# One VectorE pass of an attention kernel takes over the clamp, and the weighed values reach x by way of GpSimd

## The chip, the cores and the metric

The kernel runs on one core of one Trainium2 chip, as a single launch. The metric is the device time of that core in microseconds (us); lower is better. The time before the change is the median of three runs.

## The reference

x has 8 sequences of 512 tokens of 128 features. The reference computes x + 0.5 FFN(LN(x)), then x + Attention(LN(x)), then x + 0.5 FFN(LN(x)) again. The FFN is a mixture of 8 experts, two of them chosen per token. Only the attention matters here. It has 16 heads with complex queries and keys of 64 dimensions, turned by a phase. For a query i and a key j of a head, with dt = |i - j|:

```
E      = exp(clip(-mu * dt, -30, 0))
s      = Re(q_i . conj(k_j));  qn = |q_i|^2;  kn = |k_j|^2
V      = sigma_sq / (2 mu) * (1 - E*E) + eta_sq + gamma_sq
maha   = max(qn + E*E*kn - 2*E*s, 0) / V
logits = coef * log1p(maha / nu) - 0.5 * DH * log(V)      (masked where j > i)
out    = softmax(logits) @ v,   x = x + out @ Wo
```

## The kernel before, in words

There are three stages: a dense stage (an FFN, and preparation for the attention), the attention, and a second dense stage. All of them are written by hand for five queues (TensorE, VectorE, ScalarE, GpSimd and the SyncE queue, which issues the DMAs), with semaphores between them. On each queue the order is the order of the program text.

The attention stage walks through 128 pairs of a head and a sequence, head by head, eight sequences per head. Every queue has a function `a_step(i, r)`, called for steps -1 to 132; in step n = 16 i + r it works on several pairs at different depths of the pipeline. The score matrix of a pair is 512 x 512, of which only the lower triangle of 128 x 128 blocks is kept: four row blocks of 128, 384, 512 and 256 columns (in this order in memory), 1280 columns for each of the 128 partitions. In step n:

- TensorE: scores of pair n into `pS` (`scores`, L1186), norms of pair n+1 (`norms`), the projections of pair n+2 into `pQK` (`project`), the transposes of the probabilities of pair n-1 back into `pS` (`turn`, L1226; its two halves wait for the two halves of `t_done` of pair n, since they overwrite the same `pS`), in every second head the values for two heads (`values`, L1236), then the product of probabilities and values of pair n-2 into `p7` (`weigh`, L1300, which waits for `acc_done`, since `p7` is a single buffer).
- VectorE: `peaks` of pair n-1 (L1569: four instructions at L1578 that add `lam` and take the row minimum), the first half of `accumulate` of pair n-3 (L1603: x += p7 * rinv, two of four row tiles, L1609), `distances` of pair n (L1583: a pass pS = -2 pS + ek, L1587, and a second one u = pS * decay in two instructions of 512 and 768 columns, L1591), the transpose of the query norms of pair n+1 (L1597), the other half of `accumulate`, the phase products of pair n+2 (`turn_parts`, L1631 and L1633), and the reciprocal of the row sums of pair n-1 (L1601). In some steps it also builds tables for the next head. For the last head, `moments` (L1614) follows the second half of `accumulate` in steps 123 to 130: it takes the statistics of the new x, and waits for `acc_done` of that pair.
- ScalarE: `soften` of pair n-1 (exponentials), `key_norms` of pair n+1 (knorm = kn + a constant, L1384), `clamp` of pair n (L1386: Relu with a bias `qnorm` for each row, four instructions at L1392), `turned_out` of pair n-1 (copy of the transposes, L1399), `logs` of pair n (L1401: two instructions at L1405), `square` of pair n+2, and in every second head `values_out`.
- GpSimd: `rotate` of pair n+1 (L1495, one add over 1024 columns, after `s_done` of pair n and after a DMA that SyncE issues for `crossed`), `spread` of pair n+1 (L1502: ek = decay * knorm in four instructions at L1509, which waits for `w_done` of pair n, the end of the first pass, since `ek` is a single buffer), and `query_norms` of pair n+1 (L1512, one instruction on 4 columns).

So before the change the pair's distance is built as (-2 s + E kn) * E; the clamp and the query norm are added on ScalarE, and the logarithm follows there in a second visit.

Of the kernel before, what the change touches and what calls it, by code (L numbers as in the profile page):

```python
# [28 lines left out]
P = 128  # L29
# [13 lines left out]
HIGHEST = 3.0e38  # L43

# [3 lines left out]
SW = 1280  # L48
# [59 lines left out]
def dense_phase(nc, s, layer):  # L108
# [6 lines left out]
    with ExitStack() as ctx:  # L115
# [177 lines left out]
        def _(pe):  # L293
# [57 lines left out]
            def down(e):  # L351
# [4 lines left out]
                pe.wait_ge(lo_done, e + 1)  # L356
                if k == 0:
                    wait(pe, x_done, c - 1)
                    pe.wait_ge(xlo_done, turned_before(e))
# [277 lines left out]
        def _(g):  # L637
# [13 lines left out]
            if first:  # L651
                weights_low(0)
                weights_low(1)
                weights_low(2)
                down_low(0)
                down_low(1)
            for e in range(SLOTS):
# [385 lines left out]
def attention_phase(nc, s):  # L1043
# [4 lines left out]
    with ExitStack() as ctx:  # L1048
        sb = lambda name, shape, dt=F32: ctx.enter_context(nc.sbuf_tensor(name, shape, dt))
        sem = lambda name: ctx.enter_context(nc.semaphore(name))  # L1050
        decay = (s.decay0, sb("decay1", [P, SW]))
# [5 lines left out]
        decay2, wqk_raw, by_cos, by_sin, crossed = s.decay2, s.wqk_raw, s.by_cos, s.by_sin, s.crossed  # L1057
        squares, rot, knorm, u, z = s.squares, s.rot, s.knorm, s.u, s.z
        qnorm = sb("qnorm", [P, 2, TILES])
        q_turned = sb("q_turned", [P, 2, P])  # L1060
# [3 lines left out]
        val_even = [sb(f"val_even{k}", [P, N]) for k in range(3)]  # L1064
# [19 lines left out]
        def far(h):  # L1084


            return decay[h % 2][:, span(TILES - 1)] if h % 2 or h == 0 else s.far_even

# [53 lines left out]
        def _(sp):  # L1142
# [14 lines left out]
            def expand(h):  # L1157
# [4 lines left out]
                wait(sp, S["t_done"], 2 * (h - 1) * B)  # L1162
# [22 lines left out]
        def _(pe):  # L1185
# [114 lines left out]
            def weigh(i, r):  # L1300
# [4 lines left out]
                wait(pe, S["acc_done"], n)  # L1305
# [50 lines left out]
        def _(a):  # L1356
            def build(part, h):
# [4 lines left out]
                elif part == LN:  # L1362
                    if h == 0:
                        a.wait_ge(S["decay_done"], 1)
                        a.activation(decay2[:], far(0), ACT.Square).then_inc(S["decay2_done"], 1)
                    a.wait_ge(S["decay2_done"], h + 1)
                    wait(a, S["zred_done"], 2 * (h - (1 if h % 2 else 3)) * B)
                    a.activation(lam(h), decay2[:], ACT.Ln, bias=hp(h, A_PLUS_B), scale=hp(h, NEG_A)).then_inc(S["lnv_done"], 1)
# [17 lines left out]
            def clamp(i, r):  # L1386
                n = i * 16 + r
                wait(a, S["qn_done"], n + 1)
                for k, (_, pieces) in enumerate(HALVES):
                    wait(a, S["t_done"], 2 * n + k + 1)  # L1390
                    for I in pieces:
                        last = a.activation(u[:, span(I)], u[:, span(I)], ACT.Relu, bias=qnorm[:, r % 2, I:I + 1])  # L1392
                    last.then_inc(S["relu_done"], 1)

# [6 lines left out]
            def logs(i, r):  # L1401
                n, h = i * 16 + r, i * 2 + r // B
                for k, (half, _) in enumerate(HALVES):
                    a.wait_ge(S["relu_done"], 2 * n + k + 1)
                    a.activation(u[:, half], u[:, half], ACT.Ln, bias=hp(h, U_MIN)).then_inc(S["ln_done"], 1)  # L1405
# [39 lines left out]
            def a_step(i, r):  # L1445
# [18 lines left out]
                if live(i, r):  # L1464
                    clamp(i, r)
                if live(i, r - 1):
                    turned_out(i, r - 1)
                if live(i, r):
                    logs(i, r)
# [19 lines left out]
        def _(g):  # L1489
# [12 lines left out]
            def spread(i, r):  # L1502
                n, par = i * 16 + r, parity(r)
                wait(g, S["decay_done"], i * 2 + r // B + 1)
                wait(g, expanded[par], 48 * (i + r // 16 + 1) if par else 64 * (i + r // 16))
                wait(g, S["norm_done"], n + 1)
                wait(g, S["w_done"], n)
                for I in ORDER:
                    last = g.tensor_tensor(ek[:, span(I)], decay[par][:, span(I)], knorm[:, 0:(I + 1) * P], ALU.mult)  # L1509
                last.then_inc(S["ek_done"], 1)  # L1510

            def query_norms(i, r):  # L1512
                n, h = i * 16 + r, i * 2 + r // B
                wait(g, S["qt_done"], n + 1)
                wait(g, S["relu_done"], 2 * (n - 1))
                column = q_turned[:, r % 2].rearrange("p (c d) -> p c d", c=TILES)[:, :, 0]
                g.tensor_scalar(qnorm[:, r % 2, :], column, hp(h, NEG_NU_A), None, ALU.subtract).then_inc(S["qn_done"], 1)

            def a_step(i, r):
                if live(i, r + 1):  # L1520
# [3 lines left out]
                    query_norms(i, r + 1)  # L1524
                if i == 0 and r == -1:
                    build_first()

# [3 lines left out]
        def _(v):  # L1531
            def build_front(h):
                if h % 2:
                    wait(v, S["norm_done"], (h - 1) * B)
# [364 lines left out]
```

## Time and profile before

| what | value |
|---|---|
| time, median of 3 runs (lowest to highest) | 1684.14 us (1682.43 to 1686.3) |
| profiled execution, its own time | 1685.38 us |
| span of the profiled execution | 1683.6 us |
| busy: TensorE / VectorE / ScalarE / GpSimd | 1624.1 / 1494.5 / 1443.1 / 1013.6 us |
| first and last L1587 (pairs 0 and 127) start at | 260.80 us and 1455.08 us |

Positions in the trace are counted from the start of the span. The profiled execution's own time is 1.8 us more than its span. A row of the timeline gives the start, the duration, the engine, the line, the operation, the tile written, the tiles read with their shapes, and how many instructions of the same kind are merged into it ("x4"); in square brackets stands how long the engine had been idle before it, and what ended that. In a group of the view by line, the number after the comma is the mean duration of one instruction in ns. PEld is TensorE's loading of weights, POOL is GpSimd, DVE is VectorE and ACT is ScalarE.

### The profile page before, as it was taken

The numbers are of one execution on the slowest core, as the hardware profiler recorded it, in microseconds if no ns is written. First come the engines' busy times: TensorE is split into PE (matmuls) and PEld (weight loads), VectorE is DVE, ScalarE is ACT, GpSimd is POOL, SyncE is SP. The second block draws the span as 40 slices with busy tenths as digits, with TensorE's granted clock in tenths as the row PEclk, the third lists the DMA queues.
The fourth block names the chain that finished last, engine by engine and source line by source line (L and its number), as shares of the span: only waits on it lengthen the run. The fifth ranks groups of instructions, "written<-read, shape, count | busy, mean of one in ns | idle before, by whom it ended". The sixth has DMA issues, their size and how long they took to land. (4 is left out here: it accounts for less than half of the span.)

```text
span 1683.6 us, 31247 instructions
## 1 busy us (share of the span) xinstructions
PE 1624.1 (96%) x9690; PEld 1227.8 (73%) x9690; DVE 1494.5 (89%) x3380; ACT 1443.1 (86%) x2909; POOL 1013.6 (60%) x954
## 2 busy tenths in 40 slices
PE   5999988999999999999999999999999999899998
PEld 4787865777776777677777777777776776677876
DVE  6878878999999999999999999999999989977665
ACT  6677678999999999999999999999999998765765
POOL 3564556666666666665766666666666656245555
PEclk9999999999999999999999999999999999999999
DMA  6000022232223323232222323232232322100000
GB/s 178 1 1 1 1 97 73 64 92 64 76 70 76 79 64 85 58 82 70 75 74 64 92 64 76 55 92 69 74 84 60 80 59 51 26 8 7 13 13 13
DMA packets 50484, 100.05 MB, mean 59 GB/s; under 512 B 8208, under 2 KB 25872, under 8 KB 50320
## 3 DMA queue, kind: packets, MB, share of 16 engines
q1 hardware_dynamic: 50320, 98.07, 22.7%
q8 instruction: 78, 1.28, 0.3%
q14 instruction: 86, 0.70, 0.1%
HBM read 17.95 MB, written 5.24 MB: 14 GB/s over the span
## 5 line engine op out<-in xcount | busy, mean ns | idle before, releaser
L1500 POOL TENSOR_TENSOR early<-early 128x1024 f32<-128x1024 f32 x127 | 303.7, 2391 | 421.4 <-PE pS L1191 227.6
L661 POOL TENSOR_TENSOR hid_lo_d<-hid_d,hid_hi_d 128x512 fp32r<-128x512 f32 x176 | 231.4, 1315 | 218.4 <-ACT hid_hi_d L566 211.8
L1392 ACT ACTIVATE early<-early,qnorm 128x128 f32<-128x128 f32 (+3 forms) x512 | 246.6, 552 | 68.0 <-DVE early L1591 67.3
L1191 PE MATMUL pS<-early 128*128 128x128 f32 (+3 forms) x1024 | 297.6, 433 | 0.4 <-PEq L115 0.4
L1376 ACT ACTIVATE early<-early,nmax 128x128 f32<-128x128 f32 (+3 forms) x512 | 280.9, 558 | 7.7 <-DVE nmax L1578 7.4
L1191 PEld LDWEIGHTS pS<-early 128*128 128x128 f32 x1024 | 164.7, 191 | 96.1 <-issue 61.4
L1587 DVE SCALAR_TENSOR_TENSOR pS<-pS,ek 128x1280 f32<-128x1280 f32 x128 | 190.9, 1492 | 43.5 <-PE pS L1191 41.9
L1509 POOL TENSOR_TENSOR ek<-early 128x128 f32<-128x128 f32 (+3 forms) x256 | 216.1, 877 | 3.0 <-ACT early L1384 2.6
L1509 POOL TENSOR_TENSOR ek<-decay,early 128x128 f32<-128x128 f32 (+3 forms) x256 | 215.0, 873 | 0.0
L1233 PE MATMUL pS<-ident,early 128*128 128x128 f32 x1280 | 184.9, 278 | 13.3 <-DVE early L1591 7.0
L1405 ACT ACTIVATE early<-early,params 128x512 f32<-128x512 f32 (+1 forms) x256 | 196.4, 816 | 0.0
L1233 PEld LDWEIGHTS pS<-ident,early 128*128 128x128 f32 x1280 | 143.5, 141 | 62.1 <-DVE early L1591 32.1
L566 ACT ACTIVATE hid_hi_d<-hid_d 128x512 fp32r<-128x512 f32 x176 | 111.1, 631 | 60.8 <-DVE hid_d L794 43.0
L1399 ACT ACTIVATE probT<-pS 128x1280 f32<-128x1280 f32 x128 | 155.9, 1218 | 3.4 <-PE pS L1233 3.4
L1311 PE MATMUL p<-val_odd,probT 128*128 128x128 f32 x1280 | 156.9, 278 | 1.3 <-ACT probT L1399 1.3
L1311 PE MATMUL p<-val_even,probT 128*128 128x128 f32 x1280 | 154.4, 276 | 0.0
L1311 PEld LDWEIGHTS p<-val_odd,probT 128*128 128x128 f32 x1280 | 147.9, 192 | 6.0 <-ACT probT L1399 1.6
L1609 DVE SCALAR_TENSOR_TENSOR x_sb<-p,rinv,x_sb 128x128 f32<-128x128 f32 x512 | 149.4, 332 | 1.3 <-PE p L1311 1.3
L1311 PEld LDWEIGHTS p<-val_even,probT 128*128 128x128 f32 x1280 | 148.1, 192 | 1.5
L1578 DVE CUSTOM_DVE_ANT_0 early<-early,lam,params 128x128 f32<-128x128 f32 (+3 forms) x256 | 133.6, 575 | 8.8 <-issue 0.5
L1204 PE MATMUL pV<-early,ones 128*128 128x512 f32 x254 | 131.1, 598 | 4.4 <-ACT val_odd L1418 3.9
L1411 ACT ACTIVATE early<-pQK 128x1024 f32<-128x1024 f32 x127 | 127.6, 1005 | 1.8 <-DVE early L1633 1.8
(393 smaller groups left out, 3752.5 us busy)
## 6 DMA issues: line engine op xcount, KB each, us to landing
early<-early SPq DMA_DIRECT2D x263, 256.0 KB, 3.4
early<-trig_d SPq DMA_DIRECT2D x64, 64.0 KB, 2.0
trig_d<-early SPq DMA_DIRECT2D x3, 1024.0 KB, 6.9
early<-in_w SPq DMA_DIRECT2D x3, 704.0 KB, 8.7
x_sb<-in_x SPq DMA_DIRECT2D x4, 512.0 KB, 8.3
early<-in_wqk SPq DMA_DIRECT2D x16, 128.0 KB, 3.4
cos<-trig_d SPq DMA_DIRECT2D x32, 64.0 KB, 2.2
sin<-trig_d SPq DMA_DIRECT2D x32, 64.0 KB, 2.0
```

What stands on the lines that cost most here:

```text
L661: g.tensor_tensor(hid_lo[:, par], hid[:, par], hid_hi[:, par].bitcast(F32), ALU.subtract).then_inc(lo_done, 1)
L1191: last = pe.matmul(s.pS[:, span(I)], rot[:, I * P:(I + 1) * P], rot[:, N:N + (I + 1) * P], start=True, stop=True)
L1233: last = pe.transpose(s.pS[:, col:col + P], z[:, col:col + P], s.ident[:])
L1311: last = pe.matmul(s.p7[:, I * P:(I + 1) * P], turned[:, OFF[I] + J * P:OFF[I] + (J + 1) * P], val[:, J * P:(J + 1) * P], start=(J == 0), ...
L1376: last = a.activation(z[:, span(I)], z[:, span(I)], ACT.Exp, bias=nmax[:, I:I + 1], scale=-1.0, accum_out=rsum[:, r % 4, I:I + 1])
L1392: last = a.activation(u[:, span(I)], u[:, span(I)], ACT.Relu, bias=qnorm[:, r % 2, I:I + 1])
L1399: a.activation(probT[r % 2][:], s.pS[:, 0:SW], ACT.Copy).then_inc(S["trc_done"], 1)
L1405: a.activation(u[:, half], u[:, half], ACT.Ln, bias=hp(h, U_MIN)).then_inc(S["ln_done"], 1)
L1500: g.tensor_tensor(rot[:], by_cos[:], crossed[:], ALU.add).then_inc(S["rot_done"], 1)
L1509: last = g.tensor_tensor(ek[:, span(I)], decay[par][:, span(I)], knorm[:, 0:(I + 1) * P], ALU.mult)
L1587: v.scalar_tensor_tensor(s.pS[:, 0:SW], s.pS[:, 0:SW], -2.0, ek[:], ALU.mult, ALU.add).then_inc(S["w_done"], 1)
L1609: last = v.scalar_tensor_tensor(xt, s.p7[:, I * P:(I + 1) * P], rinv[:, r % 4, I:I + 1], xt, ALU.mult, ALU.add)
```

## The change

1. The distance is built as (-2 s) * E in the first pass, which reads `decay` and no longer `ek`; the second pass adds `ek`, now E*E*kn, and takes the maximum with a lower bound `low` for each row. It is four VectorE instructions (TENSOR_ADD_SAT, with a scalar for each row) instead of two.
2. `ek` is read by the second pass, so `spread` of pair n waits for `t_done` of pair n-1 instead of `w_done`. It reads a squared decay of 512 columns instead of `decay`.
3. The clamp leaves ScalarE. `logs` takes four instructions instead of two, with `base` as its bias for each row, and stands where the clamp stood.
4. GpSimd's `query_norms` has three instructions on 4 columns, each waiting for the one before.
5. VectorE's `accumulate` becomes `normalise_out`, one product over 512 columns from `p7` into `weighed`, all of it ahead of `distances`; it waits until GpSimd has added the pair before. GpSimd's new `accumulate` adds `weighed` to x, at the end of its step. TensorE's `weigh` waits for `y_done`, the product's semaphore. `moments` waits for GpSimd's add.
6. To make room, the lower halves of the second FFN's weights (`w2_lo`) are written to DRAM in the first dense stage, and read back at the end of step 123; both DMAs are issued by GpSimd.

```diff
 def spread(i, r):
-    wait(g, S["decay_done"], i * 2 + r // B + 1)
-    wait(g, expanded[par], 48 * (i + r // 16 + 1) if par else 64 * (i + r // 16))
+    wait(g, S["decay2_done"], h + 1)
     wait(g, S["norm_done"], n + 1)
-    wait(g, S["w_done"], n)
+    wait(g, S["t_done"], 2 * n)
     for I in ORDER:
-        last = g.tensor_tensor(ek[:, span(I)], decay[par][:, span(I)], knorm[:, 0:(I + 1) * P], ALU.mult)
+        last = g.tensor_tensor(ek[:, span(I)], decay2(h)[:, near(I)], knorm[:, 0:(I + 1) * P], ALU.mult)
     last.then_inc(S["ek_done"], 1)
...
 def query_norms(i, r):                      # GpSimd
     wait(g, S["qt_done"], n + 1)
-    wait(g, S["relu_done"], 2 * (n - 1))
-    g.tensor_scalar(qnorm[:, r % 2, :], column, hp(h, NEG_NU_A), None, ALU.subtract).then_inc(S["qn_done"], 1)
+    wait(g, S["ln_done"], 2 * (n - 1))
+    at_ = base[:, r % 2, :], floor[:, r % 2, :], low[:, r % 2, :]
+    g.tensor_scalar(at_[0], column, hp(h, NEG_NU_A), hp(h, U_MIN), ALU.subtract, ALU.add).then_inc(S["base_done"], 1)
+    g.wait_ge(S["base_done"], n + 1)
+    g.tensor_scalar(at_[1], at_[0], LEAST, hp(h, U_MIN), ALU.mult, ALU.max).then_inc(S["floor_done"], 1)
+    g.wait_ge(S["floor_done"], n + 1)
+    g.tensor_tensor(at_[2], at_[1], at_[0], ALU.subtract).then_inc(S["qn_done"], 1)
+
+def accumulate(i, r):                       # GpSimd, called with r - 3 after query_norms(i, r + 1)
+    g.wait_ge(S["y_done"], n + 1)
+    g.tensor_tensor(xb, xb, weighed[:], ALU.add).then_inc(S["acc_done"], 1)
+
+def restore():                              # GpSimd, at the end of step 123
+    g.wait_ge(S["ek_done"], (H - 1) * B)
+    g.wait_ge(S["lnv_done"], H - 1)
+    g.wait_ge(S["av_done"], (H - 1) * B)
+    g.dma_start(s.w2s[1][:], s.w2_low_d).then_inc(S["w2_back"], 16)
...
 def distances(i, r):                        # VectorE
+    v.wait_ge(S["decay_done"], i * 2 + r // B + 1)
+    wait(v, expanded[par], 48 * (i + 1) if par else 64 * i)
     wait(v, S["s_done"], n + 1)
-    wait(v, S["ek_done"], n + 1)
-    v.scalar_tensor_tensor(s.pS[:, 0:SW], s.pS[:, 0:SW], -2.0, ek[:], ALU.mult, ALU.add).then_inc(S["w_done"], 1)
+    v.scalar_tensor_tensor(s.pS[:, 0:SW], s.pS[:, 0:SW], -2.0, decay[par][:, 0:SW],
+                           ALU.mult, ALU.mult).then_inc(S["w_done"], 1)
     wait(v, S["w_done"], n + 1)
+    v.wait_ge(S["ek_done"], n + 1)
+    v.wait_ge(S["qn_done"], n + 1)
     wait(v, S["zred_done"], 2 * n)
-    for half, _ in HALVES:
-        v.tensor_tensor(u[:, half], s.pS[:, half], decay[par][:, half], ALU.mult).then_inc(S["t_done"], 1)
+    for _, pieces in HALVES:
+        for I in pieces:
+            last = v._custom_dve(bass.dve_ops.TENSOR_ADD_SAT, out=u[:, span(I)], in0=s.pS[:, span(I)],
+                                 in1=ek[:, span(I)], s0=HIGHEST, s1=low[:, r % 2, I:I + 1])
+        last.then_inc(S["t_done"], 1)
...
-def accumulate(i, r, tiles=range(TILES)):   # VectorE
-    for I in tiles:
-        xt = s.x_sb[:, b * TILES + I, :]
-        last = v.scalar_tensor_tensor(xt, s.p7[:, I * P:(I + 1) * P], rinv[:, r % 4, I:I + 1], xt,
-                                      ALU.mult, ALU.add)
-    if TILES - 1 in tiles:
-        last.then_inc(S["acc_done"], 1)
+def normalise_out(i, r):                    # VectorE, called with r - 3 ahead of distances(i, r)
+    v.wait_ge(S["av_done"], n + 1)
+    v.wait_ge(S["rinv_done"], n + 1)
+    wait(v, S["acc_done"], n)
+    v.tensor_tensor(weighed[:], s.p7.rearrange("p (c d) -> p c d", c=TILES),
+                    rinv[:, r % 4, :].unsqueeze(2).broadcast_to([P, TILES, P]), ALU.mult).then_inc(S["y_done"], 1)
...
-def clamp(i, r):                            # ScalarE: Relu, four instructions, with qnorm as the bias
 def logs(i, r):
-    for k, (half, _) in enumerate(HALVES):
-        a.activation(u[:, half], u[:, half], ACT.Ln, bias=hp(h, U_MIN)).then_inc(S["ln_done"], 1)
+    for k, (_, pieces) in enumerate(HALVES):
+        a.wait_ge(S["t_done"], 2 * n + k + 1)
+        for I in pieces:
+            last = a.activation(u[:, span(I)], u[:, span(I)], ACT.Ln, bias=base[:, r % 2, I:I + 1])
+        last.then_inc(S["ln_done"], 1)
```

## Rows read from the trace of the kernel before

**Rows 1.** The page: busy time, share of the span and instructions of each engine.

```profile
PE 1624.1 (96%) x9690; PEld 1227.8 (73%) x9690; DVE 1494.5 (89%) x3380; ACT 1443.1 (86%) x2909; POOL 1013.6 (60%) x954
```

**Rows 2.** Busy time by stretch, attention; the last three are clock, DMA share, GB/s.

```profile
299.00:1414.70 1115.70, 1106.58 (x7160) 824.93 (x7159) 1058.75 (x2357) 1048.94 (x2180) 717.09 (x714) 1.00 0.29 73
```

**Rows 3.** Timeline, VectorE: first pass of pairs 4, 65, 66, 123 and 127.

```profile
301.71 1.50 DVE L1587 SCALAR_TENSOR_TENSOR pS<-pS,ek 128x1280 f32<-128x1280 f32 x1 [0.52 <-PE pS L1191]
...
870.69 1.50 DVE L1587 SCALAR_TENSOR_TENSOR pS<-pS,ek 128x1280 f32<-128x1280 f32 x1 [0.98 <-PE pS L1191]
...
880.55 1.50 DVE L1587 SCALAR_TENSOR_TENSOR pS<-pS,ek 128x1280 f32<-128x1280 f32 x1 [0.93 <-PE pS L1191]
...
1414.72 1.49 DVE L1587 SCALAR_TENSOR_TENSOR pS<-pS,ek 128x1280 f32<-128x1280 f32 x1
...
1455.08 1.49 DVE L1587 SCALAR_TENSOR_TENSOR pS<-pS,ek 128x1280 f32<-128x1280 f32 x1
```

**Rows 4.** Timeline, TensorE's weight loads: the second half of a turn.

```profile
873.83 0.64 PEld L1233 LDWEIGHTS pS<-ident,early 128*128 128x128 f32 x6 [0.18 <-DVE early L1591]
```

**Rows 5.** Timeline, VectorE: pieces of two steps without values.

```profile
804.73 0.48 DVE L1578 CUSTOM_DVE_ANT_0 early<-early,lam,params 128x128 f32<-128x128 f32 x1
...
805.14 0.61 DVE L1578 CUSTOM_DVE_ANT_0 early<-early,lam,params 128x384 f32<-128x384 f32 x1
...
806.35 0.48 DVE L1578 CUSTOM_DVE_ANT_0 early<-early,lam,params 128x256 f32<-128x256 f32 x1
...
810.27 0.30 DVE L1597 STREAM_TRANSPOSE q_turned<-pV 128x128 f32<-128x128 f32 x1
...
810.99 1.21 DVE L1631 TENSOR_TENSOR early<-pQK,sin 128x1024 f32<-128x1024 f32 x1
812.12 1.21 DVE L1633 TENSOR_TENSOR early<-pQK,cos 128x1024 f32<-128x1024 f32 x1
813.25 0.17 DVE L1601 RECIPROCAL rinv<-rsum 128x4 f32<-128x4 f32 x1
...
813.83 1.07 DVE L1578 CUSTOM_DVE_ANT_0 early<-early,lam,params 128x384 f32<-128x384 f32 x1
```

**Rows 6.** Timeline, ScalarE: clamp and logs of one pair.

```profile
1408.33 1.92 ACT L1392 ACTIVATE early<-early,qnorm 128x128 f32<-128x128 f32 x4 [0.83 <-DVE early L1591]
...
1411.28 1.53 ACT L1405 ACTIVATE early<-early,params 128x512 f32<-128x512 f32 x2
```

**Rows 7.** Groups by line and shape, VectorE, 600 to 1400 us.

```profile
L1609 DVE SCALAR_TENSOR_TENSOR x_sb<-p,rinv,x_sb 128x128 f32<-128x128 f32 x342 | 99.8, 331 | 0.0
...
L1591 DVE TENSOR_TENSOR early<-pS,decay 128x768 f32<-128x768 f32 x42 | 39.8, 947 | 0.0
...
L1591 DVE TENSOR_TENSOR early<-pS,decay 128x512 f32<-128x512 f32 x42 | 29.0, 691 | 1.5
```

**Rows 8.** Timeline, GpSimd: a longer L1517, and one whole step.

```profile
814.48 0.59 POOL L1517 TENSOR_SCALAR qnorm<-q_turned,params 128x4 f32<-128x4 f32 x1
...
870.83 2.38 POOL L1500 TENSOR_TENSOR early<-early 128x1024 f32<-128x1024 f32 x1 [3.38 <-PE pS L1191]
873.17 3.37 POOL L1509 TENSOR_TENSOR ek<-early 128x128 f32<-128x128 f32 x4
876.52 0.30 POOL L1517 TENSOR_SCALAR qnorm<-q_turned,params 128x4 f32<-128x4 f32 x1
```

**Rows 9.** Timeline, second dense stage: 512 columns on VectorE (from PSUM) and on GpSimd.

```profile
1478.57 0.68 DVE L786 TENSOR_TENSOR gated_d<-pS,early 128x512 f32<-128x512 f32 x1
...
1488.71 1.30 POOL L661 TENSOR_TENSOR hid_lo_d<-hid_d,hid_hi_d 128x512 fp32r<-128x512 f32 x1 [0.77 <-ACT hid_hi_d L566]
```

**Rows 10.** Timeline, VectorE: the moments of step 123.

```profile
1418.55 0.87 DVE L1618 BATCH_NORM_STATS2 stats_at<-x_sb 128x6 f32<-128x128 f32 x4
1419.45 0.38 DVE L1622 BATCH_NORM_AGGREGATE mv<-stats_at 128x2 f32<-128x6 f32 x4
```

**Rows 11.** DMA issues: KB each, median us to landing.

```profile
early<-in_w SPq DMA_DIRECT2D x3, 704.0 KB, 8.7
```

More of the change, by code:

```diff
@@ L356, in down @@
                 pe.wait_ge(lo_done, e + 1)
+                if last_phase and e == 0:
+                    pe.wait_ge(s.S["w2_back"], 16)
                 if k == 0:
@@ L1050, in attention_phase @@
         sem = lambda name: ctx.enter_context(nc.semaphore(name))
+        square_even = tuple(sb(f"square_even{k}", [P, N])[:] for k in range(2))
+        val_even = [sb(f"val_even{k}", [P, N]) for k in range(3)]
         decay = (s.decay0, sb("decay1", [P, SW]))
@@ L1464, in a_step @@
                 if live(i, r):
-                    clamp(i, r)
+                    logs(i, r)
                 if live(i, r - 1):
                     turned_out(i, r - 1)
-                if live(i, r):
-                    logs(i, r)
                 if i == 0 and r in (0, 1):
@@ L1556, in build_square @@
                 v.wait_ge(S["lnv_done"], h)
-                v.tensor_tensor(decay2[:], far(h), far(h), ALU.mult).then_inc(S["decay2_done"], 1)
+                wait(v, S["ek_done"], (h - (1 if h % 2 else 3)) * B)
+                v.tensor_tensor(decay2(h), far(h), far(h), ALU.mult).then_inc(S["decay2_done"], 1)
             def build_back(h):
@@ L1742, in a_step @@
                     if live(i, r - 3):
[L1743 removed]
+                        normalise_out(i, r - 3)
                     distances(i, r)
@@ L1749, in a_step @@
                     query_norms(i, r + 1)
-                if live(i, r - 3) and n != PAIRS:
-                    accumulate(i, r - 3, range(TILES // 2 if live(i, r) else 0, TILES))
+                if live(i, r - 3) and n > PAIRS:
+                    normalise_out(i, r - 3)
                 if n == PAIRS:
@@ L1848, in program @@
         s.silu1 = part(2 * N).rearrange("p (a t) -> p a t", a=2)
-        dense_phase(nc, s, 0)
+        w2_low = lambda n: nc.sbuf_tensor(f"w2_lo{n}", [P, HC * P], F32R)
+        with w2_low(0) as first:
+            s.w2s = (w2_hi, first)
+            dense_phase(nc, s, 0)
+        with w2_low(1) as again:
+            s.w2s = (w2_hi, again)
         attention_phase(nc, s)
-        dense_phase(nc, s, 1)
+        with w2_low(2):
+            dense_phase(nc, s, 1)
 def kernel(**inputs):
```

63 lines of the change are left out of this document (33 added, 30 removed).

## The prediction

> **What bounds the kernel now.** I read the page first [rows 1]: three engines are busy for 86 to 96% of the span and GpSimd for 60%, so no share by itself names the bound. The busy time by stretch shows the attention's steady part alone [rows 2]: TensorE 1106.6, VectorE 1058.8, ScalarE 1048.9 and GpSimd 717.1 of 1115.7 us, at the full granted clock (1.00, the 2.4 GHz level). GpSimd is the only engine with room. Then I read the timeline, with the first VectorE pass as the clock of the loop [rows 3]. Pair 4 starts it at 301.71, pair 123 at 1414.72: 119 steps in 1113.0 us, 9.35 on average. A step with values takes 9.86 (870.69 to 880.55), and VectorE was idle for 0.93 to 0.98 ahead of it, waiting for the scores. There TensorE's own chain ends last: scores, two VectorE passes, second half of the turn (it waited 0.18 for VectorE [rows 4]), values, product, next scores. 60 of the 119 steps are of this kind, so the 59 others average (1113.0 - 60 x 9.86) / 59 = 8.84. In those VectorE has no idle time before the pass (pair 123's row has none): it is the bound. Two exact clocks, then: TensorE's loop in half of the steps, VectorE's in the other half, and GpSimd in neither.
>
> **VectorE's edits.** The first pass keeps its 1.50 [rows 3]. The second has four instructions where two took 0.69 and 0.95 [rows 7]; the two rows differ by 0.256 for 256 columns, 1.0 ns a column, so an instruction has a fixed 0.18, of which the next hides some 0.1. Two more instructions cost at least 2 x 0.07. At most they cost 2 x 0.2 (the fixed part of L1609: 0.331 less 0.13 for its columns). I take +0.26, near the middle, so 1.73 in all. Four L1609 at about 0.25 each (0.331 less the overlap) become one product of 512 columns from PSUM: nearest row 0.68 [rows 9], 0.60 with overlap. VectorE's work per step is -1.0 + 0.6 + 0.26, about -0.15.
>
> **ScalarE's edits.** The clamp's 1.92 and the logs' 1.53 [rows 6] become one visit of about 1.92. That is 1.5 us of ScalarE work per step, but `turned_out` stands where it stood in time, and ScalarE does not bound a step: the gain is the VectorE wait for the logs, at most 0.3 (813.25 + 0.17 to the next peaks), which is lost in what follows.
>
> **TensorE's loop** (steps with values) has the second pass in it: 9.86 + 0.26 = 10.12. What hides the rest of VectorE's work there is the idle 0.95, so no VectorE gain counts.
>
> **GpSimd's edits, and the new loop.** GpSimd worked 2.38 + 3.37 + 0.30 in a step [rows 8]. It gets two small dependent instructions more (0.3 each and 0.1 for each wait; bounds 0.6 and 1.0, nothing being able to hide them, since each waits for the one before) and an add over 512 columns, 1.30 [rows 9]. The sum, 8.2, would fit in a step. But the waits close a circle. `spread` of pair n+1 now waits for the end of the second pass of pair n; the add of pair n-3 stands behind `spread` and the three small instructions; VectorE's next product waits for that add, and stands ahead of the passes of pair n+1. So from one end of the second pass to the next:
>
> wait 0.1 + spread 3.37 + small ones 1.1 + add 1.30 + wait 0.1 + product 0.60 + first pass 1.52 + second pass 1.73 = 9.8 us.
>
> The handoffs are estimates from the 0.03 to 0.2 between a row that releases and the one released (the rotation starts 0.14 after the first pass that waits for the same scores [rows 3, 8]). On the direct way VectorE needs only transpose 0.24, phase products 2.26, reciprocal 0.1, peaks 2.0 and these three, 8.5 [rows 5]: it would stand still for over a microsecond in front of the product.
>
> **Collisions.** In the circle the peaks run from 2.7 to 4.8 us after the second pass, and the small GpSimd instructions from 3.5 to 4.6: they now always meet. The trace has this meeting: the 384-column peak took 1.07 instead of 0.61 [rows 5] while GpSimd was in its last spread, and the small instruction took 0.59 instead of 0.30 [rows 8] under that peak. Slower peaks cost nothing here (VectorE has the microsecond); slower small ones do. Between 0 and 1.0 per step (three small ones and the add, each behind a peak); I take 0.5, three meetings at 0.3, half of them hit. The circle is then 10.3. That is above 10.12, so it sets both kinds of step: 119 x 10.3 - 1113.0 = +113.
>
> The Trainium skill, "SBUF — State Buffer", section "Who interferes with whom", says that a VectorE instruction with two SBUF inputs and a GpSimd instruction that reads SBUF exclude each other for the whole instruction. By it the peaks collide and the new second pass (one input in PSUM) does not; the rows so far agree for the peaks.
>
> **The last head.** In steps 123 to 126 `moments` (0.87 and 0.38 [rows 10]) waits for GpSimd's add of the same pair, while the phase products are queued behind it on VectorE, and behind these the transfer, the rotation and all of the next step. The add comes 0.1 + 3.37 + 1.1 + 1.3 + 0.1 = 6.0 after the second pass, VectorE is ready after 0.24: 5.7 idle in each of four steps, less 0.15 of VectorE's saving: 4 x 5.5 = +22 over the 40.4 us that pairs 123 to 127 took (1414.72 to 1455.08). In step 127 GpSimd has no spread, and the add is early.
>
> **DMAs.** GpSimd issued none before. Storing `w2_lo` falls in the first dense stage, ahead of GpSimd's first subtraction: 0 to 1 us, hidden by its idle time, I take 0. Reading it back is 704 KB, 8.7 us to landing for that size [rows 11], at the end of step 123 with tens of microseconds to its use; it may delay one transfer for a rotation: 0 to 8.7, I take 0, because VectorE stands still there for 5.7 in any case. Expansion and `build_square` get other waits, on events over a step old: nothing.
>
> **Sum.** 1685.4 (the profiled execution; its span is 1683.6, with 1.8 around it) + 113 + 22 = 1820. That execution is 1.2 above the median of the runs, so I forecast 1819. Bounds: with no collision and short handoffs the circle is 9.65, steps with values stay at TensorE's 10.12: 60 x 10.12 + 59 x 9.65 = 1176.6, +64, tail +20: 1768. With 10.8 in every step, +172, tail +25 (some of the read back): 1881.
>
> **Rivals.**
> - Full exclusion: every small instruction and the add wait for a whole peak (0.54, 0.67, 0.41 between their starts, less what is over when they arrive), about +1.0: circle 10.85, 119 x 10.85 - 1113 = +178, and +22: 1884. For it: the two long rows. Against: the spread that met a peak was not visibly longer, and the small one gained only 0.29. Chance 0.20. The rule of the Trainium skill's page named above, read strictly, is this case.
> - The circle is 9.3 (GpSimd's small ones overlap, and no peak meets them), and the last head hides half of its wait: TensorE's loop 60 x 0.26 = +16, steps without values 59 x 0.46 = +27, last head +11: 1738. Against: the spread alone is 3.37 and cannot shrink. Chance 0.07.
> - Faster: the place is the steps without values. If VectorE's product doesn't have to wait there (GpSimd's add done by 4.8 us after the second pass, where I have 6.0), the step falls from 8.84 by 0.15 + 0.3 for the logs' wait, and four instructions cost what two did: 59 x 0.45 = -27, the last head +10: 1667. It decides at a spread-to-add chain of 4.6 us; the rows add up to 5.8. Chance 0.06.
> - The second pass does not do what it says at the price of a plain one: the custom instruction runs at half the rate, +1.3 per step in the circle: 119 x 1.3 on top, 1974. The peaks are custom too, and their 384 columns take 0.61, full rate. Chance 0.05.
>
> The forecast keeps 0.62. The range leaves out the last three and a bit of the first: 1765 to 1884. A measurement of this kernel tells about 0.2% (3.4 us) from no change: faster 0.06, the same 0.02, slower 0.92.
>
> **What would show it.** Right: first-pass starts of one and the same distance, near 10.3, in steps with and without values; VectorE idle for about 1 us before the product, released by GpSimd's add; TensorE and ScalarE both with idle time in all steps; GpSimd near 8.2 + collisions busy per step; idle of 5 to 6 us before the moments four times. Wrong: two different distances, with the product never waiting for GpSimd; or spreads that start well before the second pass ends; or second-pass pieces of over twice their columns in ns.

## The result, and the profile after

The changed kernel takes 1918.38 us (median of 4 runs, 1916.07 to 1922.05) against 1685.22 us before (4 runs beside it, 1682.43 to 1687.19): a ratio of 1.1387, 95% interval 1.1361 to 1.1413. The profiled execution is the one of 1916.07, its span 1914.3. The forecast was 1819, with a range to 1884: the direction was right, the size was not.

The page of the changed kernel, which answers to [rows 1]:

```profile
PE 1680.0 (88%) x9690; PEld 1255.5 (66%) x9690; DVE 1573.1 (82%) x3252; ACT 1306.0 (68%) x2653; POOL 1371.2 (72%) x1340
```

Only GpSimd's share rose. Three engines had less idle time before; now all four have some, which is what a circle of waits looks like in a page of shares. The busy time of the steady part, from the first pass of pair 4 to that of pair 123 (it answers to [rows 2]; the last three numbers are clock, DMA share and GB/s):

```profile
302.40:1619.00 1316.60, 1153.20 (x7154) 846.85 (x7151) 1132.94 (x2229) 919.84 (x1934) 1052.82 (x1072) 0.97 0.24 61
```

VectorE is busy for 1132.9 of 1316.6 us and GpSimd for 1052.8, so neither is the bound by itself. The stretches of the span come from four rows of VectorE's timeline, the first passes of pairs 4, 123 and 127 (against [rows 3]) and the moments of step 123 (against [rows 10]):

```profile
302.45 1.49 DVE L1611 SCALAR_TENSOR_TENSOR pS<-pS,early 128x1280 f32<-128x1280 f32 x1
...
1619.05 1.49 DVE L1611 SCALAR_TENSOR_TENSOR pS<-pS,decay 128x1280 f32<-128x1280 f32 x1
...
1628.32 0.87 DVE L1645 BATCH_NORM_STATS2 stats_at<-x_sb 128x6 f32<-128x128 f32 x4 [5.59 <-POOL x_sb L1537]
...
1681.50 1.48 DVE L1611 SCALAR_TENSOR_TENSOR pS<-pS,decay 128x1280 f32<-128x1280 f32 x1
```

Up to pair 4: +0.7 us. The 119 steps to pair 123: 1316.6 for 1113.0, +203.6. Pairs 123 to 127: 62.45 for 40.36, +22.1, with the stall of 5.59 in front of the moments. After pair 127: 232.8 for 228.5, +4.3. Together +230.7, the difference of the two spans.

So nearly nine tenths of the loss are in the steady steps: 11.06 us on average for 9.35. Here is one whole step with values, first VectorE, then GpSimd. In it VectorE also builds a piece of a table for the next head (L1559, 0.68 us, between the phase products and the peaks):

```profile
809.09 0.69 DVE L1638 TENSOR_TENSOR weighed<-p,rinv 128x512 f32<-128x512 f32 x1 [1.41 <-POOL x_sb L1537]
809.70 1.49 DVE L1611 SCALAR_TENSOR_TENSOR pS<-pS,early 128x1280 f32<-128x1280 f32 x1
811.22 1.92 DVE L1619 CUSTOM_DVE_ANT_0 early<-pS,ek,low 128x128 f32<-128x128 f32 x4
...
820.08 0.69 DVE L1638 TENSOR_TENSOR weighed<-p,rinv 128x512 f32<-128x512 f32 x1 [1.41 <-POOL x_sb L1537]
820.68 1.49 DVE L1611 SCALAR_TENSOR_TENSOR pS<-pS,early 128x1280 f32<-128x1280 f32 x1
```

```profile
813.31 3.57 POOL L1512 TENSOR_TENSOR ek<-square_even,early 128x128 f32<-128x128 f32 x4 [1.86 <-DVE early L1619]
816.87 0.81 POOL L1527 TENSOR_SCALAR base<-dist,params 128x4 f32<-128x4 f32 x1
817.77 0.65 POOL L1529 TENSOR_SCALAR floor<-base,params 128x4 f32<-128x4 f32 x1
...
818.67 1.27 POOL L1537 TENSOR_TENSOR x_sb<-x_sb,weighed 128x512 f32<-128x512 f32 x1
820.06 2.38 POOL L1504 TENSOR_TENSOR early<-early 128x1024 f32<-128x1024 f32 x1
```

Follow it from the first pass at 809.70 to the next at 820.68. The second pass ends at 813.14. GpSimd had been idle for 1.86, released by it, and starts the spread at 813.31. The three small instructions run from 816.87, the add from 818.67 to 819.94. VectorE had been idle for 1.41, released by the add, and starts the product at 820.08. Each of the two engines waits for the other once a step. (In the last two steps of each head with values, 14 of the 119, VectorE's own work is longer and the product follows the last peak with no idle time.) A step without values is the same circle. Here is one of 10.95, from 765.87 to 776.82, again VectorE and then GpSimd:

```profile
765.87 1.49 DVE L1611 SCALAR_TENSOR_TENSOR pS<-pS,decay 128x1280 f32<-128x1280 f32 x1
...
772.22 1.07 DVE L1601 CUSTOM_DVE_ANT_0 early<-early,lam,params 128x384 f32<-128x384 f32 x1
...
776.21 0.69 DVE L1638 TENSOR_TENSOR weighed<-p,rinv 128x512 f32<-128x512 f32 x1 [1.82 <-POOL x_sb L1537]
776.82 1.49 DVE L1611 SCALAR_TENSOR_TENSOR pS<-pS,decay 128x1280 f32<-128x1280 f32 x1
```

```profile
769.49 3.39 POOL L1512 TENSOR_TENSOR ek<-early 128x128 f32<-128x128 f32 x4 [2.03 <-DVE early L1619]
772.86 1.21 POOL L1527 TENSOR_SCALAR base<-dist,params 128x4 f32<-128x4 f32 x1
774.17 0.38 POOL L1529 TENSOR_SCALAR floor<-base,params 128x4 f32<-128x4 f32 x1
...
774.79 1.28 POOL L1537 TENSOR_TENSOR x_sb<-x_sb,weighed 128x512 f32<-128x512 f32 x1
```

The 384-column peak (1.07 for 0.61) and GpSimd's first small instruction (1.21) meet here. The same instruction in step 123, where VectorE stands still in front of the moments and no peak is near, takes 0.39, and the three together end 1.04 after the first began:

```profile
1625.98 0.39 POOL L1527 TENSOR_SCALAR base<-dist,params 128x4 f32<-128x4 f32 x1
1626.48 0.31 POOL L1529 TENSOR_SCALAR floor<-base,params 128x4 f32<-128x4 f32 x1
1626.87 0.20 POOL L1531 TENSOR_TENSOR low<-floor,base 128x4 f32<-128x4 f32 x1
1627.02 1.26 POOL L1537 TENSOR_TENSOR x_sb<-x_sb,weighed 128x512 f32<-128x512 f32 x1
```

Four of the 119 steps are not set by the circle alone: the first step of heads 8, 10, 12 and 14 is 11.89 long. The next first pass, at 976.19, had to wait for the scores after the product was done:

```profile
976.19 1.50 DVE L1611 SCALAR_TENSOR_TENSOR pS<-pS,early 128x1280 f32<-128x1280 f32 x1 [0.85 <-PE pS L1202]
```

```profile
968.70:972.00 3.30, 3.30 (x17) 3.30 (x17) 3.30 (x8) 3.08 (x5) 3.30 (x4) 0.50 0.56 127
```

The second row is a stretch of that step. TensorE was busy in all of it at a granted clock of 0.50, the 1.2 GHz level; before the clock fell it had waited 1.92 and 0.33 for VectorE's second pass. In that step its product of pair n-2 took 2.91, in a step at 1.00 it takes 2.39. The first steps of heads 2, 4 and 6, at 1.00 throughout, are 10.96 to 10.97 long. So I put the difference down to the clock; no run took it apart. It comes to about 0.9 in each of the four, 3.7 us in all.

### The profile page after: what moved, and what is told of

The parts are those of the page before. It is cut to its first block and busy times, and to the rows that moved or that the text cites. A ratio compares the mean times of both kernels' runs of the same rounds, so it can differ in the third digit from the quotient of the medians.

```text
span 1914.3 us, 31134 instructions
## 1 busy us (share of the span) xinstructions
PE 1680.0 (88%) x9690; PEld 1255.5 (66%) x9690; DVE 1573.1 (82%) x3252; ACT 1306.0 (68%) x2653; POOL 1371.2 (72%) x1340
## 5 line engine op out<-in xcount | busy, mean ns | idle before, releaser
L1410 ACT ACTIVATE early<-early,base 128x128 f32<-128x128 f32 (+3 forms) x512 | 259.8, 554 | 268.9 <-DVE early L1619 258.4
L1244 PE MATMUL pS<-ident,early 128*128 128x128 f32 x1280 | 200.1, 290 | 170.1 <-DVE early L1619 170.0
L1504 POOL TENSOR_TENSOR early<-early 128x1024 f32<-128x1024 f32 x127 | 304.7, 2399 | 36.8 <-DMA early<-early 13.6
L1512 POOL TENSOR_TENSOR ek<-square_even,early 128x128 f32<-128x128 f32 (+3 forms) x256 | 224.7, 912 | 116.7 <-DVE early L1619 115.5
L1619 DVE CUSTOM_DVE_ANT_0 early<-pS,ek,low 128x128 f32<-128x128 f32 (+3 forms) x512 | 246.5, 544 | 5.8 <-POOL low L1531 1.4
L1638 DVE TENSOR_TENSOR weighed<-p,rinv 128x512 f32<-128x512 f32 x128 | 88.3, 690 | 180.4 <-POOL x_sb L1537 176.8
L1537 POOL TENSOR_TENSOR x_sb<-x_sb,weighed 128x512 f32<-128x512 f32 x128 | 172.5, 1347 | 25.5 <-DVE weighed L1638 25.5
L1322 PE MATMUL p<-val_odd,probT 128*128 128x128 f32 x1280 | 172.3, 296 | 1.3 <-ACT probT L1402 1.3
L1322 PEld LDWEIGHTS p<-val_odd,probT 128*128 128x128 f32 x1280 | 168.4, 214 | 1.8 <-ACT probT L1402 1.6
L1601 DVE CUSTOM_DVE_ANT_0 early<-early,lam,params 128x128 f32<-128x128 f32 (+3 forms) x256 | 163.8, 691 | 0.1
```

The lines of the kernel that those rows point to most:

```text
L1244: last = pe.transpose(s.pS[:, col:col + P], z[:, col:col + P], s.ident[:])
L1322: last = pe.matmul(s.p7[:, I * P:(I + 1) * P], turned[:, OFF[I] + J * P:OFF[I] + (J + 1) * P], val[:, J * P:(J + 1) * P], start=(J == 0), ...
L1410: last = a.activation(u[:, span(I)], u[:, span(I)], ACT.Ln, bias=base[:, r % 2, I:I + 1])
L1504: g.tensor_tensor(rot[:], by_cos[:], crossed[:], ALU.add).then_inc(S["rot_done"], 1)
L1512: last = g.tensor_tensor(ek[:, span(I)], decay2(h)[:, near(I)], knorm[:, 0:(I + 1) * P], ALU.mult)
L1537: g.tensor_tensor(xb, xb, weighed[:], ALU.add).then_inc(S["acc_done"], 1)
```

## The experiments

Three questions: is the circle the cause, what makes it longer than I had it, and what is each half of the change worth by itself? The table gives each run: median, ratio to the kernel before with its 95% interval, mean step with and without values (pairs 4 to 123), pairs 123 to 127, and the span after pair 127's first pass.

| kernel | us | ratio | with | without | 123 to 127 | after |
|---|---|---|---|---|---|---|
| before | 1685.2 | 1 | 9.86 | 8.83 | 40.4 | 228.5 |
| changed | 1918.4 | 1.139 [1.136, 1.141] | 11.18 | 10.94 | 62.5 | 232.8 |
| e8_two_weighed | 1765.8 | 1.047 [1.046, 1.049] | 10.55 | 9.05 | 62.5 | 233.9 |
| e1_add_ahead_of_spread | 1740.7 | 1.033 [1.031, 1.034] | 10.34 | 9.17 | 42.9 | 232.4 |
| e2_add_ahead_of_small | 1832.0 | 1.087 [1.085, 1.089] | 10.70 | 10.05 | 60.2 | 232.3 |
| e6_peaks_one_input | 1810.7 | 1.074 [1.072, 1.076] | 10.39 | 10.02 | 61.4 | 230.9 |
| e3_clamp_alone | 1742.8 | 1.034 [1.032, 1.035] | 10.37 | 9.21 | 42.8 | 228.7 |
| e7_add_early_no_clamp | 1710.1 | 1.014 [1.013, 1.016] | 10.01 | 9.02 | 42.8 | 231.9 |
| e4_add_alone | 1738.0 | 1.031 [1.030, 1.033] | 9.96 | 9.34 | 54.7 | 230.8 |
| e5_add_alone_early | 1713.5 | 1.017 [1.015, 1.020] | 9.96 | 9.08 | 42.2 | 232.1 |
| e9_product_behind_distances | 1714.8 | 1.018 [1.016, 1.020] | 9.98 | 9.18 | 40.5 | 229.0 |
| e10_sum_behind_distances | 1701.0 | 1.009 [1.008, 1.011] | 9.87 | 9.09 | 40.4 | 228.8 |

Each ratio is against the runs of the kernel before that stood beside that kernel's own.

**Is it the circle?** e8 keeps every instruction of the changed kernel and gives the product a second buffer, so that it waits for the add of the pair before last:

```diff
-weighed = sb("weighed", [P, TILES, P])
+weighed = sb("weighed", [P, 2, TILES, P])
...
-    wait(v, S["acc_done"], n)
+    wait(v, S["acc_done"], n - 1)
```

> The changed kernel with two buffers for the weighed values, so that the product of a pair waits for the add of two pairs before; the order on GpSimd is as changed. Theory 1 (the circle closes through that one buffer): it opens, steps with values 10.34, those without 9.2 to 9.4, while the moments of the last head still wait: about 1758 us. Rival (GpSimd's load and order, not the buffer): above 1850 us.

Measured 1765.8: the second buffer takes 152.6 us off. Between 600 and 1400 us the product no longer waits at all; the first row is e8's, by line, and the one under it the changed kernel's:

```profile
L1638 DVE TENSOR_TENSOR weighed<-p,rinv 128x512 f32<-128x512 f32 x82 | 55.8, 680 | 0.0
```

```profile
L1638 DVE TENSOR_TENSOR weighed<-p,rinv 128x512 f32<-128x512 f32 x73 | 50.4, 690 | 105.6 <-POOL x_sb L1537 105.6
```

The last head keeps its 62.5 us, since the moments still wait for the late add. That is the part that the buffer cannot mend, and the order can. e1 puts the add of the changed kernel ahead of the wait for the second pass, where GpSimd stood idle for nearly 2 us:

```diff
 def a_step(i, r):                # GpSimd
+    rotate(i, r + 1)
+    accumulate(i, r - 3)
-    rotate(i, r + 1)
     spread(i, r + 1)
     query_norms(i, r + 1)
-    accumulate(i, r - 3)
```

> The changed kernel with GpSimd's add of pair n-3 moved ahead of the spread (after the rotation), into the time in which the spread waits for the second pass anyway. Theory 1 (the circle second pass, spread, three small instructions, add, product, two passes sets every step): the circle loses its add and small ones, so steps with values fall back to TensorE's loop, 9.86 plus 0.4 for the longer second pass = 10.25, steps without values to about 9.2 (GpSimd's own work, 2.4 + 1.3 + 3.6 + 1.8), and the moments of the last head wait no more: about 1732 us. Theory 2 (the added work and the collisions on VectorE and GpSimd are the cost, wherever the add stands): over 1850 us, with both kinds of step still near 11.

Measured 1740.7, 8.7 above the forecast: of the 233 us, 178 are gone by a change of order alone, 156 of them in the steady steps and 19.5 in the last head. The two forms agree that the wait for the add, not the work that was moved, is most of the loss.

e2 puts the add between the spread and the three small instructions:

```diff
     spread(i, r + 1)
+    accumulate(i, r - 3)
     query_norms(i, r + 1)
-    accumulate(i, r - 3)
```

> The changed kernel with GpSimd's add between the spread and the three small instructions. Theory 1: the circle is shorter by the 1.80 of the small ones, 10.98 - 1.80 = 9.2, so steps with values go by TensorE's loop, 10.25, those without by about 9.2 to 9.4, and the moments still wait, 4 times about 4 us: about 1750 us. Theory 2: no change, above 1850 us.

A miss: 1832.0. The step with values is still 10.70. In a step of VectorE's timeline and GpSimd's beside it:

```profile
930.95 1.07 DVE L1602 CUSTOM_DVE_ANT_0 early<-early,params 128x384 f32<-128x384 f32 x1
931.95 1.75 DVE L1602 CUSTOM_DVE_ANT_0 early<-early,params 128x512 f32<-128x512 f32 x1
933.62 0.48 DVE L1602 CUSTOM_DVE_ANT_0 early<-early,params 128x256 f32<-128x256 f32 x1
934.03 0.68 DVE L1639 TENSOR_TENSOR weighed<-p,rinv 128x512 f32<-128x512 f32 x1
```

```profile
931.56 1.58 POOL L1537 TENSOR_TENSOR x_sb<-x_sb,weighed 128x512 f32<-128x512 f32 x1
933.13 1.07 POOL L1527 TENSOR_SCALAR base<-dist,params 128x4 f32<-128x4 f32 x1
```

The product follows the last peak with no idle time: VectorE is the bound, and it is so because its 512-column peak took 1.75 instead of 0.74 while the add took 1.58 instead of 1.27. The 0.74 is from the kernel before:

```profile
805.68 0.74 DVE L1578 CUSTOM_DVE_ANT_0 early<-early,lam,params 128x512 f32<-128x512 f32 x1
```

I had counted slower peaks as free; here they set the step. The wait of the moments stays too, at 4.5 to 6.5 four times.

**What makes the circle longer than 10.3?** e6 leaves the circle alone and gives the peaks one SBUF input in place of two. It leaves out the term lam, the mask and the minimum of the peaks:

```diff
-last = v.tensor_tensor_reduce(z[:, span(I)], u[:, span(I)], lam(h)[:, near(I)],
-                              hp(h, NEG_COEF), HIGHEST, ALU.add, ALU.min, nmax[:, I:I + 1])
+last = v.tensor_scalar(z[:, span(I)], u[:, span(I)], 0.0, 0.0, ALU.mult, ALU.add,
+                       accum_out=nmax[:, I:I + 1])
```

> The changed kernel with the four peak instructions of each pair reading one SBUF tensor instead of two (tensor_scalar with an accumulator in place of the reduce over u + lam; lam, its mask and the minimum are left out, as are the right probabilities). Theory 1 with collisions: the peaks no longer exclude GpSimd, so the spread falls from 3.57 to 3.37 and the three small ones from 1.80 to about 1.0, the circle from 10.98 to about 10.0; steps with values stop at TensorE's 10.34: about 1812 us. Rival (the three small ones and the handoffs are simply that long, no collision): unchanged within 10 us, 1918 us.

Measured 1810.7, as expected. The timeline of one step without values, GpSimd and then VectorE:

```profile
861.14 0.39 POOL L1527 TENSOR_SCALAR base<-dist,params 128x4 f32<-128x4 f32 x1
861.63 0.32 POOL L1529 TENSOR_SCALAR floor<-base,params 128x4 f32<-128x4 f32 x1
862.03 0.20 POOL L1531 TENSOR_TENSOR low<-floor,base 128x4 f32<-128x4 f32 x1
862.18 1.27 POOL L1537 TENSOR_TENSOR x_sb<-x_sb,weighed 128x512 f32<-128x512 f32 x1
```

```profile
860.74 0.68 DVE L1601 TENSOR_SCALAR_CACHE_REDUCE early<-early 128x512 f32<-128x512 f32 x1
861.35 0.41 DVE L1601 TENSOR_SCALAR_CACHE_REDUCE early<-early 128x256 f32<-128x256 f32 x1
863.59 0.69 DVE L1637 TENSOR_TENSOR weighed<-p,rinv 128x512 f32<-128x512 f32 x1 [1.82 <-POOL x_sb L1537]
```

The peaks still run beside GpSimd's small instructions (the last two begin at 860.74 and 861.35), and these keep the 0.39, 0.32 and 0.20 that they have when VectorE stands still. The circle stays closed, with 1.82 of idle time before the product. It is 10.02 long instead of 10.95, so in a step without values the meetings cost 0.93. In one with values the mean falls by 0.79 only, 11.18 to 10.39: TensorE's 10.34 now ends the step, and the spread keeps its 3.56 there, beside L1559, which e6 leaves as it is. In all e6 takes 108 us off. By the rule of the Trainium skill, "SBUF — State Buffer", section "Who interferes with whom" (a VectorE instruction with two SBUF inputs and a GpSimd one that reads SBUF exclude each other), it would be gone with the second input, and it is: the rule and these rows agree. e6 also puts another instruction in the peaks' place, shorter by up to 0.1, so it shows that these peaks no longer meet GpSimd's instructions, not that one SBUF input is enough in general (the last section has a case where it was not).

**The clamp and the squared decay alone.** e3 is the changed kernel with the sum back on VectorE, as before, in two halves around the distances:

```diff
-normalise_out(i, r - 3)          # ahead of distances
+accumulate(i, r - 3, range(TILES // 2))
 distances(i, r)
...
+accumulate(i, r - 3, range(TILES // 2 if live(i, r) else 0, TILES))
```

> The changed kernel with x += p7 * rinv back on VectorE, in two halves as before: the clamp's part of the change alone. Theory 1: without the add on GpSimd there is no circle. Left are the longer second pass (+0.4 in each step with values, 10.25) and on VectorE 8.84 + 0.4 less the wait for the logs, about 9.0: about 1720 us, and no stall before the moments. Theory 2 (the clamp's part is the dear one, by collisions with the three small instructions): above 1800 us.

Measured 1742.8, +57 us where I expected +35. The mean step with values grew by 0.51 and the one without by 0.38. e7 is e1 with the second pass as two plain adds of 512 and 768 columns, without the lower bound:

```diff
-for _, pieces in HALVES:
-    for I in pieces:
-        last = v._custom_dve(bass.dve_ops.TENSOR_ADD_SAT, out=u[:, span(I)], in0=s.pS[:, span(I)],
-                             in1=ek[:, span(I)], s0=HIGHEST, s1=low[:, r % 2, I:I + 1])
+for half, _ in HALVES:
+    v.tensor_tensor(u[:, half], s.pS[:, half], ek[:, half], ALU.add).then_inc(S["t_done"], 1)
```

> The run with the add ahead of the spread (1740.7 us), with the second pass as two plain sums of 512 and 768 columns; the lower bound is left out. Theory 1: the four instructions with a bound are all that is left in TensorE's loop. Steps with values fall from 10.34 to 9.87, those without from 9.17 to about 8.75: about 1687 us. Rival: the steps are longer for other reasons (the second pass waits for ek and the row bounds, GpSimd's 9.1 us of work): above 1715 us.

It came out at 1710.1, between the two theories. Against e1 the four bounded instructions cost 31 us: 0.33 in a step with values, 0.15 without. If they cost the same in e3, that is about half of its loss. The other half I can only argue: with `ek` read by the second pass the spread starts later, and its small instructions fall under the peaks in e3 too (L1527 takes 0.80 to 0.82 in most steps without values, 0.56 to 1.20 in those with). No run took that apart.

**The product and the add alone.** e4 is the kernel before with VectorE's product ahead of the distances and GpSimd's add at the end of its step. e5 has the add ahead of the spread:

```diff
 def a_step(i, r):                # e4
     spread(i, r + 1)
     query_norms(i, r + 1)
+    accumulate(i, r - 3)         # e5: ahead of spread(i, r + 1)
...
-accumulate(i, r - 3, range(TILES // 2))
+normalise_out(i, r - 3)
 distances(i, r)
```

> The kernel before with only the product on VectorE and the add on GpSimd (at the end of GpSimd's step, as in the change), distances and clamp as before. Theory 1: the spread waits for the first pass only, so the circle from scores to product is about 8.2 and binds nothing; steps with values keep 9.86, those without gain 0.3 from VectorE's lighter work (-18 in all), and the moments of the last head wait about 4 us four times (+17): about 1685 us. Theory 2 (the add by itself is dear): above 1750 us.

> As the run with the add alone, but GpSimd's add stands ahead of the spread. In that run steps with values kept 9.86 to 10, those without went to 9.3 (the peaks wait 0.65 for ScalarE's logs, now that the whole product stands ahead of the distances, and the first peak collides with GpSimd's add), and pairs 123 to 127 took 54.7 us. Theory 1: only the wait of the moments goes, -14 us, the rest stays: about 1724 us. Theory 2 (the circle through the product counted in these steps too): steps without values fall to 8.6, about 1690 us.

e4 took 1738.0, a clear miss, and e5 1713.5, between the two values given for it. In neither does the spread wait for the second pass, and the product does not wait for the add; still both are slower than before. Two rows of e4, VectorE and GpSimd:

```profile
977.21 0.81 DVE L1587 CUSTOM_DVE_ANT_0 early<-early,lam,params 128x128 f32<-128x128 f32 x1 [0.65 <-ACT early L1406]
```

```profile
976.57 1.29 POOL L1524 TENSOR_TENSOR x_sb<-x_sb,weighed 128x512 f32<-128x512 f32 x1
```

The same peak in the kernel before, which starts 0.14 after the reciprocal of [rows 5] ends:

```profile
813.56 0.35 DVE L1578 CUSTOM_DVE_ANT_0 early<-early,lam,params 128x128 f32<-128x128 f32 x1
```

The two sums that stood behind the distances filled VectorE's time until the logs were there. With all of the product ahead of them, the peaks wait 0.65 for the logs instead of 0.14, and the first then meets the add (0.81 for 0.35). What e5 saves over e4 is 12.5 us in the last head, where the moments get their add earlier, and 0.13 a step.

Then the product should stand behind the distances, I thought. e9 does that and leaves the last head's sums on VectorE; e10 moves only the kernel before's own four sums there, with nothing on GpSimd:

```diff
-accumulate(i, r - 3, range(TILES // 2))
 distances(i, r)
...
-accumulate(i, r - 3, range(TILES // 2 if live(i, r) else 0, TILES))
+accumulate(i, r - 3)             # e9: normalise_out(i, r - 3)
```

> A try at a faster version: the kernel before (clamp on ScalarE), with the product on VectorE moved behind the distances, the add on GpSimd at the end of its step, and the last head's eight pairs added on VectorE as before, so that no moments wait. Theory 1 with collisions: steps with values keep 9.86; in those without, VectorE's and ScalarE's loops fall to about 8.3, but GpSimd's 7.4 us of work and the peaks exclude each other, so no step falls below about 8.9: 1685 to 1695 us. Rival (collisions are small when nothing waits for GpSimd): steps without values near 8.4, about 1662 us.

> The kernel before with all four instructions of x += p7 * rinv behind the distances, none ahead of them; nothing is put on GpSimd. In steps without values the loop from second pass over clamp, transposes, logs and peaks to the next second pass loses 0.52 us and is 8.2, VectorE's own work stays 8.5, and TensorE's product of pair n-2 may wait up to 0.4 for the sum: between 8.5 and 8.9 per step, so 1670 to 1690 us. If collisions and not VectorE's wait for the logs made 8.83 out of 8.69, nothing is gained: 1685 us.

Both missed on the slow side: 1714.8 and 1701.0. In e9's steps without values VectorE has no idle time, and one of its peaks stands beside the add, here the one of 512 columns (VectorE's row, then GpSimd's):

```profile
981.31 1.75 DVE L1587 CUSTOM_DVE_ANT_0 early<-early,lam,params 128x512 f32<-128x512 f32 x1
```

```profile
980.98 1.54 POOL L1524 TENSOR_TENSOR x_sb<-x_sb,weighed 128x512 f32<-128x512 f32 x1
```

For e10, first TensorE's rows and then VectorE's:

```profile
959.79 2.47 PE L1311 MATMUL p<-val_even,probT 128*128 128x128 f32 x20 [0.41 <-issue]
962.10 2.32 PE L1191 MATMUL pS<-early 128*128 128x128 f32 x8
```

```profile
964.46 1.50 DVE L1587 SCALAR_TENSOR_TENSOR pS<-pS,ek 128x1280 f32<-128x1280 f32 x1 [0.56 <-PE pS L1191]
```

TensorE's next product has to wait for the sum (`acc_done`) before it may write where the sum reads; the profile books the 0.41 ahead of it to issue, and that this wait is its cause I infer from the order of the code and from VectorE's timeline, where the fourth sum ends at 959.69, 0.10 ahead. The product starts later, the scores come later, and VectorE waits 0.56 for them; in the kernel before it did not wait for the scores in steps without values. All four sums behind the distances end later than two of them did. No kernel of this study beat the one before.

## Why the prediction was wrong in size

- **What bounds the kernel before, and the new circle: right.** Both kinds of step now show one and the same circle (not in the 14 and the 4 steps named above), the idle time before the product is released by GpSimd's add (1.41 and 1.82), TensorE and ScalarE have idle time in all steps, and the circle is gone when its one buffer is doubled (e8) or the add moved ahead of the wait (e1).
- **The step that failed: the length of the circle,** "The circle is then 10.3". Term by term in the step of 10.98 shown above, with the measured value behind the forecast: handoffs 0.1 + 0.1, 0.17 + 0.14; the second pass 1.73, 1.92; spread 3.37, 3.57; small ones 1.1 (1.04 without a meeting), here 1.80; add 1.30, 1.27; product 0.60, 0.60; first pass 1.52, 1.52.
- **Collisions** are the largest error: "I take 0.5", and e6 measures 0.93. The forecast took three meetings at 0.3 and counted half of them. In the step with values the small instructions take 1.80 for 1.04 and the spread 3.57 for 3.39, together 0.94; in the one without, the small ones alone lose 0.89 (772.86 to 774.79, where the add begins). One long wait under a peak is worth as much as two short ones. The 0.18 of the spread is not the peaks' but L1559's, and stays in e6. The rival "Full exclusion" had this term at 1.0. Its price was about right, and I gave it 0.20; but it let every small instruction wait for a whole peak, where the rows show one that does, and its 1884 is still 34 short. One argument against it was misread: the spread that starts at 811.04 in the trace of before, the one that met a peak, took 3.46, a tenth more than the 3.37 of [rows 8].
- **The second pass** is 0.19 above the forecast of 1.73. Before the change its two instructions ran for 1.55 from start to end, the row below; the forecast started from 1.47, the distance to the next instruction, though GpSimd waits for the end. From 1.55 to 1.92 is 0.37, for which I took 0.26 between bounds of 0.14 and 0.4. The upper bound was the one to take: e7, with 1.55 again, saves 0.33 in a step where TensorE's chain ends last.

```profile
808.80 1.55 DVE L1591 TENSOR_TENSOR early<-pS,decay 128x512 f32<-128x512 f32 x2
```

- **Longer steps,** on which the forecast had nothing, raise the mean from 10.95 to 11.06. Most of it, 0.08 a step, is in the steps with values whose pieces of a table are long: 30 steps of 11.1 to 11.4, where VectorE's longer work puts other instructions beside GpSimd's. The other 0.03 is in the four of 11.89, which build no table and wait for the scores at the lower clock.
- Together 0.43 (collisions) + 0.19 + 0.11 (handoffs) + 0.11 (longer steps) - 0.07 (spread, small ones and add without meetings) = 0.77 a step; measured are 11.06 - 10.3 = 0.76, 91 of the 96 us between the forecast sum of 1820 and the profiled execution. The other 5 lie at the two ends.
- **"Slower peaks cost nothing here": right in most steps of the changed kernel,** where VectorE has idle time (in the 14 without it a 256-column peak takes 1.48 for 0.48), and wrong where the circle is shorter (e2).
- **The last head: right,** +22.1 for +22, with 5.59 to 5.60 of idle time, four times, for 5.7.
- **The end, behind pair 127: not forecast,** +4.3. It goes with the add on GpSimd in the last head: 230.8 to 233.9 in all seven other kernels that have it there, 228.5 to 229.0 in those with the last sums on VectorE. 2.8 of it are two more waits of the moments for that add, 1.38 and 1.41; no kernel with the last sums on VectorE has them. The first:

```profile
1700.15 0.88 DVE L1645 BATCH_NORM_STATS2 stats_at<-x_sb 128x6 f32<-128x128 f32 x4 [1.38 <-POOL x_sb L1537]
```

- **TensorE's loop** was forecast at 10.12. Apart from the four steps at the lower clock it did not set the changed kernel's steps. e1 and e3, where the circle is out of the way, show 10.34 and 10.37, so this term too was 0.2 short; half of that is the second pass.
- **The DMAs: right,** no idle time of VectorE in the attention is put down to them. GpSimd waits 13.6 us for them in all ahead of its rotation, which the circle hides. The read back landed 4.5 us after its issue.

The sums show what the halves are worth: the clamp alone +57, the add alone +53 (or +28 in its early place), both with the add early +55, both as changed +233. With the add early the two together cost no more than the clamp alone; they do not even add up to 57 + 28. Of the 178 us between +233 and +55, 156 lie in the steady steps: no cost of either half, but of the circle that exists only when the spread waits for the second pass and the add stands behind the spread. Another 19.5 are the moments' wait for the late add, which e4 has in part without the circle.

## What to carry to other kernels

Before work goes to an engine with idle time, follow each new wait round until it comes back to its start, and put the moved instruction ahead of the wait that makes the idle time, or give its buffer a second copy; both took most of the loss away here. Where rows show instructions of two engines that lengthen each other, add them up as if they were one engine's; where tiny instructions of one always meet a train of the other's, take the high bound for them. A place on an engine that looks as if work could be moved one slot later may already be the last one that its reader can stand.

## What the runs showed of the hardware

- A GpSimd instruction on 4 columns takes 0.39 us with VectorE still and up to 1.21 beside the peaks; three that depend on one another take 1.04 in all, 1.5 to 2.1 beside the peaks and mostly 1.8 or 1.9, and 1.04 again when the peaks have one SBUF input (e6).
- It goes both ways: a 512-column peak took 1.75 instead of 0.74 behind a GpSimd add (e2).
- A VectorE instruction that reads one SBUF tensor and a scalar for each row can be lengthened too. The piece of a table that VectorE builds took 0.46 in the kernel before and 1.52 in e9, where GpSimd's add had begun 0.04 ahead of it:

```profile
886.62 0.46 DVE L1537 TENSOR_SCALAR early<-dist,params 128x512 f32<-128x512 f32 x1
```

```profile
902.27 1.52 DVE L1546 TENSOR_SCALAR early<-dist,params 128x512 f32<-128x512 f32 x1
```

```profile
902.23 1.28 POOL L1524 TENSOR_TENSOR x_sb<-x_sb,weighed 128x512 f32<-128x512 f32 x1
```

- Four bounded VectorE instructions on PSUM take 1.92 for 1280 columns, in every step read here, beside GpSimd's instructions or not; the two plain ones before took 0.69 and 0.95 [rows 7], together 1.55.
- The changed kernel, in which TensorE has more idle time, shows a granted clock of 0.97 in the steady part, the kernel before 1.00. The mean is made of stretches of about 3.4 us at the lower level (0.50) and the rest at 1.00. Of the 21 between pair 4 and pair 123, 17 fall in steps that are no longer for it; the four in the first step of heads 8, 10, 12 and 14 come with a wait for the scores. e1, e3, e7 and e8 show 1.00 between 600 and 1400 us.
